# Heads of 32: the quotient one step behind the sums, units in pairs, and the side bank lent to a unit

## The reference

```python
xn = _ln(x, lnx_g, lnx_b)
yn = _ln(y, lny_g, lny_b)
q = jnp.einsum('bsc,hcd->bhsd', xn, wq)
k = jnp.einsum('btc,hcd->bhtd', yn, wk)
v = jnp.einsum('btc,hcd->bhtd', yn, wv)
a = jax.nn.softmax(jnp.einsum('bhsd,bhtd->bhst', q, k) * D ** (-0.5), axis=-1)
o = jnp.einsum('bhst,bhtd->bhsd', a, v)
o = o.transpose(0, 2, 1, 3).reshape(x.shape[0], x.shape[1], H * D)
x_out = x + o @ li1_w + li1_b
```

## Time and profile before

| | |
|---|---|
| median of 3 executions | 8027.38 us (8024.2 to 8045.86) |
| the profiled execution | 8022.59 us |
| its span, first to last instruction | 8020.8 us |
| TensorE, VectorE, ScalarE, GpSimd busy | 89%, 74%, 62%, 29% of the span |
| mean granted clock of TensorE | 0.94 |
| stage "own", first to last exp | 3239.2 to 3795.4 us |
| stage "cross", first to last exp | 4017.6 to 6173.6 us |

### The profile page before, as it was taken

One profiled execution on the slowest core, in us unless ns is written; L12 is line 12 of the kernel. 1 busy time (PEld: TensorE's weight loads), 2 busy tenths in 40 slices (PEclk: granted clock), 3 DMA queues, 4 the chain that ended last, 5 costly groups with the idle time before them and its releaser, 6 DMA issues. The chain is left out here.

```text
span 8020.8 us, 186125 instructions
## 1 busy us (share of the span) xinstructions
PE 7135.1 (89%) x73814; PEld 3142.3 (39%) x73814; DVE 5918.4 (74%) x12885; ACT 4951.6 (62%) x9846; POOL 2313.2 (29%) x2368
## 2 busy tenths in 40 slices
PE   6999999878999997888599999999998779999979
PEld 2333333353333333444244444444444533333335
DVE  6888888657989996677466666666665469899855
ACT  4778887636888884444255555555554248888852
POOL 1222222111121110444245444544444211221200
PEclk9999999888999998788699999999999779999989
DMA  4444333114433421000100000000000144434400
GB/s 97 101 95 92 83 83 92 45 26 100 99 89 77 99 65 31 15 16 13 53 6 8 7 6 10 6 10 6 7 3 18 49 83 96 96 84 85 97 22 14
DMA packets 319828, 417.80 MB, mean 52 GB/s; under 512 B 56533, under 2 KB 238053, under 8 KB 318968
## 3 DMA queue, kind: packets, MB, share of 16 engines
q1 hardware_dynamic: 317432, 405.36, 22.4%
q10 hardware_dynamic: 1536, 0.53, 0.0%
HBM read 225.41 MB, written 174.66 MB: 50 GB/s over the span
## 5 line engine op out<-in xcount | busy, mean ns | idle before, releaser
L687 ACT ACTIVATE a_probs<-scores_ps 128x512 f32<-128x512 f32 (+2 forms) x5248 | 2821.7, 591 | 356.2 <-PE scores_ps L607 263.4
L746 DVE TENSOR_REDUCE a_unit_max<-bank 128x1 f32<-128x512 f32 x3072 | 2004.0, 684 | 182.0 <-PE bank L594 147.3
L624 PE MATMUL bank<-a_probs,a_v_sb 128*9 128x256 f32 (+1 forms) x20992 | 1614.1, 379 | 29.4 <-ACT a_out_sb L694 20.4
L1275 ACT ACTIVATE cross_probs<-scores_ps 128x512 f32<-128x512 f32 (+1 forms) x1792 | 869.4, 571 | 772.6 <-PE scores_ps L1172 772.6
L1357 DVE TENSOR_REDUCE cross_unit_max<-bank 128x1 f32<-128x512 f32 x1536 | 1006.5, 687 | 319.7 <-PE bank L1158 316.9
L607 PE MATMUL scores_ps<-a_stack 64*128 64x256 bf16 (+1 forms) x10496 | 1131.5, 275 | 61.6 <-ACT a_probs L687 55.8
L1441 POOL TENSOR_TENSOR cross_added<-cross_probs 128x1024 f32<-128x1024 f32 x384 | 902.4, 2350 | 944.6 <-PE bank L1205 868.8
L746 DVE TENSOR_REDUCE a_unit_max<-scores_ps 128x1 f32<-128x512 f32 x1536 | 1050.2, 684 | 162.1 <-PE scores_ps L594 144.6
L594 PE MATMUL bank<-a_stack 63*128 63x512 bf16 (+2 forms) x3413 | 1039.7, 372 | 8.1 <-DMA a_stack<-a_stack_dram 2.6
L607 PEld LDWEIGHTS scores_ps<-a_stack 64*128 64x128 bf16 (+1 forms) x10496 | 373.5, 96 | 991.9 <-ACT a_probs L687 832.8
L594 PE MATMUL scores_ps<-a_stack 63*128 63x512 bf16 (+2 forms) x1707 | 635.9, 373 | 50.8 <-DMA a_stack<-a_stack_dram 47.5
(11 more groups left out here) (421 smaller groups left out, 10119.5 us busy)
## 6 DMA issues: line engine op xcount, KB each, us to landing
a_stack_dram<-a_parts SPq DMA_DIRECT2D x288, 400.2 KB, 4.3
a_stack<-a_stack_dram SPq DMA_DIRECT2D x256, 348.2 KB, 8.0
a_stack<-a_stack_dram SPq DMA_DIRECT2D x128, 444.2 KB, 9.9
a_ctxT<-in_ctxT SPq DMA_DIRECT2D x48, 400.2 KB, 4.9
a_stack_dram<-a_parts SPq DMA_DIRECT2D x288, 64.0 KB, 2.7
a_stack_dram<-a_parts SPq DMA_DIRECT2D x96, 128.0 KB, 2.8
f_x<-x_after_dram SPq DMA_DIRECT2D x32, 256.0 KB, 3.6
x_after_dram<-a_res SPq DMA_DIRECT2D x48, 128.0 KB, 4.6
```

The source lines that it names most:

```text
L624: ins = pe.matmul(out_bank[32 * h:32 * h + V8, q0:TOK], v[0:n, e.t, 4 * e.g + h, :], A.probs[0:n, held, o + q0:o + TOK], start=(e.t == 0), ...
L687: act.activation(by_pair(A.probs[0:n, b, a * 512:(a + 1) * 512])[:, :, q0:TOK], by_pair(score_bank[(2 * e.i + a) % 3][0:n, :])[:, :, q0:TO ...
L746: ins = dve.tensor_reduce(unit_max[:, e.g % 2, qt, 2 * a + j, c:c + 1], bank[:, 0:e.s.chunks[c][1]], AX.X, ALU.max)
L1275: act.activation(probs[0:n, b, h, 0:m, :].rearrange("p m q -> p (m q)"), score_bank[h][0:n, 0:m * TOK], ACT.Exp, scale=scale).then_inc(S[" ...
```

## The change

Three things, all in the list of events and the banks that it names:

1. The quotient. "norm" no longer stands right behind "take". It is held and put into the next step, behind the first units and ahead of pv. In "own" the last quad's "norm" stays where it was.
2. Pairs. In "cross" units stand in pairs: one pair (part 0) between scores and pv, one (part 2) after sums; the step with the tail units has a third pair (part 1) after pv. A quad's 28 units are now 4, 4, 2, 4, 4, 4 and 6 over seven steps (`PAIRS32`). Side work moves behind pv (slot 1), one piece per step at most apart from the ends: the second half of k in a quad's first step, v in the third and the fourth, the first half of k in the fifth, q in the sixth, turn in the seventh. The output projection moves from the fourth step of a batch to the end of its third. The LayerNorm of the context moves up by some steps, its turning down.
3. The lent bank. In "cross" the first unit of part 0 uses `side_bank`, unless side work stands directly ahead of it. The unit then waits for the side work before it to be copied out, and the next side work waits for the unit's maximum. The other units take, of the two banks, the one used longer ago.

A unit of "cross" now also waits for its q's cast, not for k's alone. The load of a batch waits for the context turns of the batch before in that buffer.

The rest of the diff only puts `e.bank`, `e.given` and `e.use` in place of `e.u % 2`, `e.u - 1` and `e.u // 2 + 1` on TensorE and VectorE.

```diff
@@ -838,6 +839,8 @@
 D32 = 32
 LAG32, BUFS32, ADDS32 = 2, 4, 2
 LN_PIECES = 5
+PAIRS32 = ((-1, ((0, 0), (2, 2))), (0, ((0, 4), (2, 6))), (1, ((0, 8),)), (2, ((0, 10), (2, 12))), (3, ((0, 14), (2, 16))),
+           (4, ((0, 18), (2, 20))), (5, ((0, 24), (1, 26), (2, 22))))
 AHEAD32 = ("ln1", "ln2", "ln3", "ln4", "ln_stats", "ln_rstd", "ln_apply", "ctx", "x_turned")
 SIDE32 = ("turn", "qk", "q", "k", "v", "ctx", "x_turned", "proj")
 
@@ -899,47 +902,57 @@
     else:
         if with_ahead:
             for j in range(LN_PIECES):
-                put((4, 5, 11, 12, 12)[j], 1, "ln_stats", j=j)
-                put((14, 15, 16, 17, 18)[j], 2, "ln_apply", j=j)
-            put(12, 2, "ln_rstd")
-            for j in range(2):
-                put(20 + j, 0, "ctx", j=j)
-            put(23, 0, "x_turned")
-        for j, (i, slot) in enumerate(((4, 0), (8, 0), (8, 2), (11, 0), (15, 0), (15, 2), (22, 0))):
-            prepare(i, slot, True, "v", j=j)
+                put((0, 4, 5, 6, 6)[j], 1, "ln_stats", j=j)
+                put(8 + j, 2, "ln_apply", j=j)
+            put(6, 2, "ln_rstd")
+            put(15, 1, "ctx", j=0)
+            put(19, 2, "x_turned")
+            put(22, 1, "ctx", j=1)
+        for j, i in enumerate((3, 9, 10, 16, 17, 23, 24)):
+            prepare(i, 1, True, "v", j=j)
         for quad in range(1, QUADS + 1):
             g, base, nxt = quad % QUADS, per_quad * (quad - 1), quad == QUADS
-            prepare(base - 3, 2, nxt, "q", g=g)
-            for c in range(2):
-                prepare(base - 2, 2 * c, nxt, "k", g=g, c=c)
-            slots = [i for i, n in ((-1, 5), (0, 5), (2, 5), (3, 5), (4, 4), (5, 4)) for _ in range(n)]
-            for k in range(s.NU):
-                prepare(base + slots[k], 0, nxt, "unit", g=g, k=k, r=int(k == s.NU - 1))
-            prepare(base + 6, 0, nxt, "turn", g=g)
-        proj_at = (3, 2)
+            prepare(base - 3, 1, nxt, "k", g=g, c=0)
+            prepare(base - 2, 1, nxt, "q", g=g)
+            prepare(base, 1, nxt, "k", g=g, c=1)
+            for rel, places in PAIRS32:
+                for part, first in places:
+                    for k in (first, first + 1):
+                        prepare(base + rel, 0, nxt, "unit", g=g, k=k, part=part, r=int(k == PAIRS32[-1][1][-1][1] + 1))
+            prepare(base + 6, 1, nxt, "turn", g=g)
+        proj_at = (2, 2)
     if with_tail:
         put(*proj_at, "proj")
 
-    plan, zero = [Ev("begin")], cur * n_steps
+    plan, zero, held = [Ev("begin")], cur * n_steps, []
     last = max([n_steps - 1] * with_core + [LAG32 - 1] * with_tail + [i for i, _ in at] + list(units_at))
     for i in range(last + 1):
         units, k = units_at.get(i, []), i - LAG32
         if with_core and i < n_steps:
             plan.append(Ev("scores", s=s, g=steps[i][0], j=steps[i][1], i=zero + i))
-        first = 1 if any(e.kind in "kv" and not s.own for e in at.get((i, 0), [])) else 2
-        plan += at.get((i, 0), []) + units[0:first]
+        by_part = [[e for e in units if e.part == part] for part in range(3)]
+        if not s.own and by_part[0] and not any(e.kind in SIDE32 for e in at.get((i - 1, 2), []) + at.get((i, 0), [])):
+            by_part[0][0].lent = True
+        plan += at.get((i, 0), []) + by_part[0] + held
+        held = []
         pv = with_core and 0 <= k < n_steps - LAG32 or with_tail and -LAG32 <= k < 0
         if pv:
             plan.append(Ev("pv", s=s, g=steps[k][0], j=steps[k][1], i=zero + k))
-        plan += units[first:first + 1] + at.get((i, 1), [])
+        plan += by_part[1] + at.get((i, 1), [])
         if pv:
             plan.append(Ev("sums", s=s, g=steps[k][0], j=steps[k][1], i=zero + k))
             if steps[k][1] == per_quad - 1:
-                plan += [Ev("take", g=steps[k][0], i=zero + k), Ev("norm", g=steps[k][0], i=zero + k)]
-        plan += units[first + 1:]
+                plan.append(Ev("take", g=steps[k][0], i=zero + k))
+                norm = Ev("norm", g=steps[k][0], i=zero + k)
+                if s.own and steps[k][0] == QUADS - 1:
+                    plan.append(norm)
+                else:
+                    held.append(norm)
+        plan += by_part[2]
         if with_core and i < n_steps:
             plan.append(Ev("mix", s=s, g=steps[i][0], j=steps[i][1], i=zero + i))
         plan += at.get((i, 2), [])
+    plan += held
     for e in plan:
         e.cur = cur
         e.batch = cur
@@ -959,19 +972,26 @@
 
     plan = [e for cur in range(-2, BATCH + 1) for e in segment32(s, cur)]
     n = u = casts = takes = 0
+    used, uses = [0, 0, 0], [0, 0, 0]
     side, cast, rows, summed, added = {}, {}, {}, {}, {}
     for e in plan:
         if e.kind == "begin":
-            e.after = side.get(("x_turned", 0, e.cur + 1))
+            e.after = side.get(("x_turned" if s.own else "ctx", 0, e.cur + 1))
         if e.kind == "ln4":
             e.after = side.get(("x_turned", 0, e.batch - 1))
         if e.kind in SIDE32:
             e.n = n
+            e.back = used[2]
             n += 1
             side[e.kind, e.g, e.batch] = n
         if e.kind == "unit" or not s.own and (e.kind == "k" or e.kind == "v" and 2 * e.j + 1 < s.T):
+            e.bank = 2 if e.lent else int(used[1] < used[0])
+            e.given, e.jobs, e.free = used[e.bank], n, None
+            uses[e.bank] += 1
+            e.use = uses[e.bank]
             e.u = u
             u += 1
+            used[e.bank] = u
         if e.kind in ("q", "k"):
             e.cast = casts = casts + 1
             cast[e.g, e.batch, e.kind, e.c] = casts
@@ -980,6 +1000,8 @@
         if e.kind == "unit":
             h, qt, c = s.unit32(e.k)
             e.cast = cast[e.g, e.batch, "k", c // 2]
+            if not s.own:
+                e.cast = max(e.cast, cast[e.g, e.batch, "q", 0])
             e.last = e.r == 1
             if e.last:
                 rows[e.g, e.batch] = len(rows) + 1
@@ -1047,12 +1069,12 @@
         w_out = sb("w_out", [P, QUADS, C])
         L = LnMem(sb, QT if own else T + QT)
         score_bank = [G.S4[:, h // 2, h % 2, :] for h in range(4)]
-        out_bank, side_bank, max_bank = G.bank[0], G.bank[1], G.bank[2:4]
+        out_bank, side_bank, max_bank = G.bank[0], G.bank[1], G.bank[2:4] + G.bank[1:2]
         n_tiles = T + QT
         ln_piece = [range(n_tiles * j // LN_PIECES, n_tiles * (j + 1) // LN_PIECES) for j in range(LN_PIECES)]
 
         S = Sems(nc, ctx, stage, ["x_in", "ctx_in", "ahead_in0", "ahead_in1", "x_res_in", "x1", "x1_out", "ln_stats", "ln_done", "side_ps",
-                                  "side_done", "cast", "max_scores0", "max_scores1", "max_taken", "max_rows", "scores0",
+                                  "side_done", "cast", "max_scores0", "max_scores1", "max_scores2", "max_taken", "max_rows", "scores0",
                                   "scores1", "scores2", "scores3", "probs", "added", "kept", "sums", "heads_out", "normed",
                                   "x_out", "dve_own", "ln_minus", "ln_shift"] + LN_SEMS)
 
@@ -1143,11 +1165,13 @@
             for e in plan:
                 if e.kind == "unit":
                     h, qt, c = s.unit32(e.k)
-                    bank = max_bank[e.u % 2]
+                    bank = max_bank[e.bank]
                     if e.cast:
                         pe.wait_ge(S["side_done" if own else "cast"], e.cast)
-                    if e.u >= 2:
-                        pe.wait_ge(S["max_taken"], e.u - 1)
+                    if e.given:
+                        pe.wait_ge(S["max_taken"], e.given)
+                    if e.lent and e.jobs:
+                        pe.wait_ge(S["side_done"], e.jobs)
                     q, k = q_of(qk_b, e), k_of(qk_b, e)
                     c0, n = s.chunks[c]
                     if qt is None:
@@ -1208,6 +1232,8 @@
                 if e.kind in SIDE32:
                     if e.n >= 1:
                         pe.wait_ge(S["side_done"], e.n)
+                    if e.back:
+                        pe.wait_ge(S["max_taken"], e.back)
                     cols = slice(e.g * P, (e.g + 1) * P)
                     m = e.batch % 2
                     if e.kind == "turn":
```

More of the change, by code:

```diff
@@ L210, in __init__ @@
         self.job, self.src, self.j, self.c, self.part, self.quad, self.r = job, src, j, c, part, quad, r
+        self.lent = False
 SPACE8 = 4
@@ L893, in segment32 @@
             for k in range(s.NU):
-                prepare(step, 0, not late, "unit", g=g, k=k, r=int(k == s.NU - 1))
+                prepare(step, 0, not late, "unit", g=g, k=k, part=max(k - 1, 0), r=int(k == s.NU - 1))
             prepare((g + 3) % QUADS, 0, g == 0, "turn", g=g)
@@ L1159, in program_pe @@
                                         start=True, stop=True)
-                    ins.then_inc(S[f"max_scores{e.u % 2}"], 1)
+                    ins.then_inc(S[f"max_scores{e.bank}"], 1)
                 if e.kind == "scores":
@@ L1228, in program_pe @@
                         c0, n = k_cols(e, 1)
```

(24 more changed lines are left out.)

## The result

The changed kernel takes 8107.7 us (median of 4, 8104.0 to 8119.7) against 8026.7 for the kernel before on the same chip: ratio 1.0098 (95% interval 1.0080 to 1.0117), 1% slower. The forecast was 7785, with 7700 to 7900 as its range.

A forecast was written before the change was run, and what follows sets the result against it. TensorE looked at its limit but was taken to wait for VectorE to free banks and for the quotient's input. Context attention -212, own attention -50, slips +20 gave -242 us: 7785 us, range 7700 to 7900.

The forecast's parts named there:

- step 2: Context attention's third step of a quad, paying for the quotient: 5.9 us with v's projection, 7.2 in the first quad.
- the 20 added for slips: Allowance for 0.1 and 0.2 us margins that fail: a third of a microsecond per quad, 64 quads, +20 us.
- Rival 3, the clock: A loop whose matmuls wait in each round can be throttled anew each round: 8109 us, chance 0.04.
- The exp floor of step 1: Context attention's second step of a quad: the loop scores, exp, scores decides its length, 3.6 us.
- v's and k's copies as what sets steps 3 and 4: Context attention: the last unit waits for VectorE's copy of the side job's odd half, 4.5 us a step.
- steps 0, 5 and 6: Context attention's first, sixth and seventh steps of a quad: 4.0, 3.75 and 3.6 us.
- the output projection's step: Step 2 of context attention's first quad: the projection waits for the quotient until 5.2, takes 1.98; 7.2 us.
- The lent bank's cover of 0.2 us: Context attention: VectorE's reduction of the side-bank unit is done at 2.3, wanted by the side job at 2.5.
- rival 1: Context attention: VectorE is late for the side bank in each step with a side job; +155, 7940 us, chance 0.14.
- the high end of the range: 7900 us, from half of rival 1, rival 2's half and the pushed exps.
- rival 2: Own attention gives nothing, as TensorE waits between the turn's cast and the third unit instead; 7835 us, chance 0.12.
- the chain of 31.7 us per batch: Own attention followed through four steps with the quotient held: 31.7 us a batch against 34.8, so -50 us.

The follow-up runs named there:

- add_waits: The changed kernel with GpSimd's addition made to wait for the quotient held into its step; 7793 us, ratio 0.9717 to the kernel before.
- after: The changed kernel itself, with held quotient, pairs and lent bank; 8107.7 us, ratio 1.0098 to the kernel before.
- held_alone: The kernel before with only the held quotient, in both stages; 8348 us, ratio 1.0415 to the kernel before.
- recip_twice: add_waits with each held quotient's reciprocal done twice; 8167 us (one run).
- no_lent: add_waits with no unit in the side bank; 7902 us, ratio 0.9850 to the kernel before.
- no_take: The changed kernel with the quotient again right behind take, without ScalarE's copy of the sums (VectorE divides out of the bank); 7675 us, ratio 0.9559 to the kernel before.

## Why the prediction was wrong

**The step that failed** is the sum of step 2: "and now come the reciprocal (1.75 us) and the product (0.43): 5.1". The product had its price from a place where no addition ran beside it. In its new place GpSimd's addition of the step starts 0.21 us before it in three quads of four, and it lasts 2.41 us; in the fourth quad it starts 1.01 us before it, and it lasts 1.61. That holds for 62 of the 64 products of context attention. Of GpSimd's casts and additions the prediction says that they "have a step of slack"; that is true, and it asked only whether GpSimd would be late, not what it does to VectorE. With the meeting taken away (add_waits) the same sum comes out: batch 121.9 for 122.6, stage 1950 for 1944, kernel 7793 for 7785. The last of the three is in part luck: of the 50 us forecast for own attention 5 came, and of the 20 added for slips context attention needed 6.

**The trace before had rows for it.** Two of the 64 products of own attention met an addition there (min/median/max ns), and 15 of the 32 additions of the output bias in context attention, which have both operands in SBUF too, last 1.11 us where the others last 0.28:

```profile
L1379 DVE TENSOR_TENSOR own_attnT<-own_out_sb,own_inv x64: 424/425/1581, 3257.7 to 3804.1; 128x256 f32<-128x256 f32 x64
L1385 DVE TENSOR_TENSOR cross_x_res<-cross_x_res,cross_b_out x32: 276/284/1116, 4171.5 to 6179.4; 128x128 f32<-128x128 f32 x32
```

The mean of the first (452 ns) hides that; the maximum doesn't. It was no bound (the product came to 2.41 us), but it told that the price depends on what runs beside it, and each step has one addition of 2.35 us. Where that lies beside the product is a matter of times, which the prediction didn't follow for GpSimd.

The Trainium skill states it ("SBUF — State Buffer", section "Who interferes with whom"): a VectorE instruction with two inputs in SBUF contends with a GpSimd instruction that reads SBUF, one in a two-port mode contends with GpSimd too, and the one that issued first blocks the other for its whole length; outside those modes an instruction with at most one SBUF input doesn't contend. The traces agree for GpSimd coming first: 2.41 us for 0.43 with two SBUF inputs, 0.42 with one. Before the change 63 of the 64 reciprocals of context attention began inside an addition and lasted 1753 ns, and 61 copies of k's half out of a bank did and kept their 425 ns; reductions that begin inside one after the change last 681 ns in the median, as the others do. That VectorE coming first blocks GpSimd is not shown by any run here.

**Rival 3, the clock**, was priced at 8109 and the kernel measured 8108; that is chance. The granted clock fell to 0.91, not to 0.84, and it fell because the stop behind the quotient grew from 1.2 to 3.2 us: three kernels have 45 stops of 3.0 to 3.2 us each (after, held_alone, recip_twice) and a clock of 0.91, 0.88 and 0.91 in the window. With a stop of 1.24 us (add_waits, third step 5.78 us) it stays at 0.99. Of the 254 us between add_waits and after in context attention, 110 are the standing itself (64 products, what they last over 0.425 us). The other 144 come with it, by recip_twice mostly at the fourth step, 7.1 for 4.56 us, whose mean granted clock is 0.60 to 0.65 in the last three quads after the change. How much of them is clock and how much queue I can't part further.

**What held.** The exp floor of step 1 (3.57, forecast 3.6), v's and k's copies as what sets steps 3 and 4 (4.56 in add_waits, 4.5), steps 0, 5 and 6 (4.07, 3.82 and 3.6 in the plain quad; 4.0, 3.75 and 3.6), the output projection's step (7.13 in add_waits, 7.2). The lent bank's cover of 0.2 us held: rival 1 didn't come. The one side job that the waits show behind a unit's reduction is the context's turning, 14 times 0.3 us in the stage.

Two sums of the prediction don't come out of their own terms. Step 5, with 3 x 0.16 to 3 x 0.31 us for its six units, gives 3.88 to 4.33 us and not 3.75; it measured 3.82. And the parts named for the high end of the range give some 7925 us and not 7900.

**Own attention** was to gain 50 us. It lost 37; in 26 of its 64 quotients the product met an addition and stood for up to 2.2 us, 52 us in all. Nearly without the meeting it takes 551 us in add_waits and 537 in no_lent, which has the same code for this stage, against 556 before: 5 to 19 us less, inside what its profiles differ by. So rival 2 is near the truth, and the chain of 31.7 us per batch was too short: measured steps (add_waits) are 8.6, 5.9, 11.8 and 9.3 (8.2, 6.3, 10.2, 7.0 forecast). It was worked out at the full clock, and the window has 0.86; how much of the difference that makes is open. That the wait for the copy of the sums bounds this stage, no_take shows (492, with the quotient in its old place).

## What to carry to other kernels

When an instruction moves, look at what other engines do at its new place, not only at who waits for it: a VectorE operation with both tensors in SBUF that begins during such an addition of GpSimd costs what is left of the latter and 0.28 us. A maximum far above the mean in its row tells that its price depends on its neighbours. See then whether one operand can come from a PSUM bank or whether GpSimd, if it has slack, can wait. And hold an instruction back only for a measured gain: here the held quotient brought none that could be told, even where it met nothing in context attention (7793 for 7792 us). On TensorE's path it isn't the length of a stop alone that counts: one grown from 1.2 to some 3 us cost 4 us per quad here, and the clock went with it.

## What the runs showed that I had not expected

- A product with two operands in SBUF that begins during a GpSimd addition of 2.35 us ends 0.28 us after it; it stood in 62 of the 64 quads of context attention (1.61 us long in the fourth of each batch, 2.41 else); beside an addition cut to a quarter it lasts 0.80 us; with one operand in a PSUM bank 0.42 us in the addition's middle.
- A tensor_scalar with one tensor operand in SBUF stands too, which fits what the Trainium skill's section above says of two-port modes (that this instruction ran in one, no trace shows): own attention's LayerNorm scaling (128 x 128) took 0.34 us alone and up to 2.10 beside an addition (min/median/max ns):

```profile
L142 DVE TENSOR_SCALAR own_x_own<-own_x,own_ln_mv,own_ln_rs x32: 334/344/2104, 3211.3 to 3755.4; 128x128 f32<-128x128 f32 x32
```

- 1.74 us of extra work on VectorE in one step of seven cost 4.1 us per quad (recip_twice), about as much as the standing product (254 / 64 = 4.0).
